# Wide maxima and full-height products in the second attention, and products of unused result in two stretches of waits

## What is computed

```
Q = query_seq @ Wq + bq;  K = ctx @ Wk + bk;  V = ctx @ Wv + bv      # 16 heads of width 16
scores = einsum('bhqd,bhkd->bhqk', Q, K) / sqrt(16)
attn = softmax(scores, axis=-1)
x = query_seq + einsum('bhqk,bhkd->bqhd', attn, V) @ Wo;  y = layernorm(x)
```

## Time and profile before

| | us |
|---|---|
| median of 3 runs (lowest, highest) | 940.2 (939.28, 941.24) |
| the profiled execution, its own time | 931.33 |
| its span, first to last instruction | 929.5 |
| TensorE busy | 847.6 (91%) |
| VectorE busy | 515.7 (55%) |
| ScalarE busy | 454.9 (49%) |
| mean granted TensorE clock | 0.965 |

### The profile page before, as it was taken

The page is one execution under the profiler, slowest core; times in us unless marked ns, Lnnn a source line. Parts: engine busy times, 40 slices in busy tenths (PEclk is TensorE's granted clock), DMA queues, the critical chain, the costliest instruction groups (busy, mean ns, idle before and its releaser), DMA issues.

```text
span 929.5 us, 10707 instructions
## 1 busy us (share of the span) xinstructions
PE 847.6 (91%) x4452; PEld 392.8 (42%) x4452; DVE 515.7 (55%) x714; ACT 454.9 (49%) x679; POOL 48.8 (5%) x41
## 2 busy tenths in 40 slices
PE   4989999989899999976899998999788989888987
PEld 2535444453434444542225435234355434554342
DVE  3479999633522012154745327359969595994442
ACT  3785222624254215334343342748885468752624
POOL 1000000300000000002100000000012000210000
PEclk9999999979999999997899899999899999999999
DMA  7000300000000000030000000000000000000011
GB/s 284 1 1 1 135 0 1 0 1 1 1 1 0 1 0 1 0 135 1 0 1 1 1 1 2 1 1 1 0 1 2 0 1 0 1 1 1 1 47 45
DMA packets 3006, 15.63 MB, mean 17 GB/s; under 512 B 656, under 2 KB 912, under 8 KB 2320
## 3 DMA queue, kind: packets, MB, share of 16 engines
q1 hardware_dynamic: 2816, 12.88, 3.5%
q0 software_dynamic: 144, 2.10, 0.6%
HBM read 12.87 MB, written 2.10 MB: 16 GB/s over the span
## 4 chain that ended last, share of the span: by engine, by line
PE 73%; ACT 14%; DVE 10%; issue 1%; DMA 1%; DVEq 0%; SPq 0%; POOL 0%; ACTq 0%
PE ps L412 71%; DVE VB L641 4%; ACT AR L628 3%; ACT AR L1822 2%; ACT AR L1812 1%; DVE AR L2118 1%; DMA CX<-in_ctxT 1%; ACT AR L1518 1%; DVE AR L653 1%; ACT AR L1788 1%; PE ps L587 1%; ACT AR L633 1%; ACT AR L631 1%; DVE AR L502 1%; ACT AR L1805 1%
## 5 line engine op out<-in xcount | busy, mean ns | idle before, releaser
L412 PE MATMUL ps<-AR,WA 128*128 128x512 f32 (+2 forms) x780 | 339.4, 596 | 5.0 <-DVE AR L2351 3.6
L412 PEld LDWEIGHTS ps<-AR,WA 128*128 128x128 f32 (+2 forms) x780 | 143.2, 189 | 187.1 <-issue 174.0
L412 PE MATMUL ps<-AR,CN 128*128 128x512 f32 (+3 forms) x320 | 113.8, 608 | 6.6 <-DVE AR L499 2.3
L412 PE MATMUL ps<-AR 128*64 128x128 f32 (+5 forms) x680 | 95.1, 401 | 9.7 <-DVE AR L2118 2.6
L653 DVE TENSOR_TENSOR AR<-ps,AR 128x512 f32<-128x512 f32 x24 | 16.6, 692 | 103.0 <-ACT AR L633 103.0
L628 ACT ACTIVATE AR<-ps 77x2048 f32<-77x2048 f32 x24 | 44.2, 1869 | 55.5 <-PE ps L412 55.3
L412 PEld LDWEIGHTS ps<-AR 128*64 128x64 f32 (+4 forms) x680 | 50.1, 158 | 46.5 <-issue 20.6
L412 PEld LDWEIGHTS ps<-AR,CN 128*128 128x128 f32 (+2 forms) x320 | 39.5, 163 | 59.0 <-issue 38.9
L641 DVE TENSOR_REDUCE VB<-ps 128x16 f32<-128x1232 f32 x32 | 44.5, 1438 | 32.3 <-PE ps L412 32.3
L412 PE MATMUL ps<-KB,WA 128*128 128x512 f32 (+1 forms) x120 | 52.9, 608 | 0.9 <-ACT AR L1805 0.9
L2248 DVE SCALAR_TENSOR_TENSOR AR<-AR,VC 128x512 f32<-128x512 f32 x72 | 50.6, 749 | 5.4 <-ACT AR L1746 4.4
(11 more groups left out here) (331 smaller groups left out, 1064.3 us busy)
## 6 DMA issues: line engine op xcount, KB each, us to landing
WA<-in_m SPq DMA_DIRECT2D x1, 2856.0 KB, 10.8
WA<-in_m SPq DMA_DIRECT2D x1, 2560.0 KB, 15.4
X<-in_xT POOLq DMA_DIRECT2D x1, 2048.0 KB, 9.1
WA<-in_m SPq DMA_DIRECT2D x1, 2048.0 KB, 9.7
out<-X SPq DMA_DIRECT2D x4, 512.0 KB, 3.1
WB<-in_m SPq DMA_DIRECT2D x1, 1024.0 KB, 5.2
AR<-in_rows SPq DMA_DIRECT2D x1, 640.0 KB, 9.8
WA<-in_m SPq DMA_DIRECT2D x1, 512.0 KB, 16.3
```

The costliest lines, as they stand in the source:

```text
L412: return nc.tensor.matmul(out, lhsT, rhs, start=first, stop=last)
```

## The change

Four edits, all on TensorE's list but one:

1. The maxima pass of "a2" takes the two zero-padded key tiles at once. A set (g, k) now covers two of the four blocks of tokens, 2k and 2k + 1, for both k of the keys: eight products of 32 rows with 154 columns in the place of sixteen with 77. VectorE's reduction reads the same 4 x 308 scores and writes its 16 results to other columns of `MXP`.
2. In that pass, from the second set on, one product of the full 128 rows with 204 columns is put between the wait for `att_mx` and the set's products. It writes the unused columns 308 to 511 of `bank(b, 0)`.
3. At the launch, three full-height products with 512 columns into bank 0 stand between the wait for the constants and that for the vectors.
4. In the second layer's head, `spare(n)` products (full height, n columns, bank 2, unused result) stand before the waits for `u5` (256, behind a wait for `kv_vs`), for `wu` (192), for `v_ln` (192) and for `ut` (256).

```
@@ attn_pe
                     else:
                         pe.wait_ge(*after("att_mx", nset(p, j, i - 1, b)))
+                        if PARTS[p] == 2:
+                            mm(bank(b, 0)[:, HALF:T], cn("ident"), CN[:, 0:T - HALF])
...
-                    for s in range(SUB):
+                    for s in range(2) if PARTS[p] == 2 else ():
+                        for r in range(4):
+                            row = slice(32 * r, 32 * r + 32)
+                            last = mm(bank(b, r)[:, 2 * s * M:2 * (s + 1) * M], qs[b][row, g, (2 * k + s) * P:(2 * k + s + 1) * P],
+                                      KF[row, :, g, b, :])
+                    for s in range(SUB) if PARTS[p] == 1 else ():
                         for r in range(4):
@@ attn_dve
-                    nc.vector.tensor_reduce(MXP[b].rearrange("p s (r n) -> p r s n", n=32)[:, :, :, i],
+                    where = MXP[b].rearrange("p s (r n) -> p r s n", n=32)
+                    nc.vector.tensor_reduce(where[:, :, :, i] if PARTS[p] == 1 else where[:, :, 2 * k:2 * k + 2, 2 * g:2 * g + 2],
@@ tensor, launch
             pe.wait_ge(*after("ld_cn", 16))
+            for n in range(3):
+                mm(ps[:, 0, :], cn("ident"), CN[:, 0:T])
             pe.wait_ge(*after("ld_vec", 16))
@@ tensor, head of the second layer
             last.then_inc(sem("h4_mm"), 1)
+
+            def spare(n):
+
+                mm(ps[:, 2, 0:n], cn("ident"), CN[:, 0:n])
+
+            pe.wait_ge(*after("kv_vs", LAYER["a2"] + 1))
+            spare(256)
             pe.wait_ge(*after("u5", 1))
             pe.wait_ge(*after("q3c", 1))
             mm(ps[:, 3, :], G6, U5).then_inc(sem("wu_mm"), 1)
+            spare(192)
             pe.wait_ge(*after("wu", 1))
...
+            spare(192)
             pe.wait_ge(*after("v_ln", 1))
             linear(0, 4)
...
             last.then_inc(sem("ut_mm"), 1)
+            spare(256)
             pe.wait_ge(*after("ut", 1))
```

## The result

| | before | after |
|---|---|---|
| median of 4 plain runs (lowest, highest), us | 939.74 (939.07, 941.24) | 931.89 (930.59, 932.25) |
| profiled execution, own time | 931.33 | 931.59 |
| its span | 929.5 | 929.8 |
| mean granted clock | 0.965 | 0.969 |

The ratio is 0.9912, 95% interval 0.9895 to 0.9929: the change takes 7.9 us off the median. The prediction had -5.1 us, to 935.1, in a range of 931.0 to 940.3.

The account below looks back on a forecast made before the run. TensorE, in flight 91% of the span, was taken to bound the kernel by its pace, clock dips and waits. Terms -0.68 - 4.00 - 2.0 + 1.6 = -5.1 us took 940.2 to 935.1 us, range 931.0 to 940.3.

Parts of the forecast that it names:

- Edit 1, the wide batch (0.55 us): Second attention's maxima pass: a wide batch takes 0.55 us against today's 0.89, so each half's first reduction starts 0.34 us sooner.
- Edit 2, the clock (-4.00 us): Second attention's first half: full-height products between sets hold the clock at 2.4 GHz, saving the dip's 4.00 us; bounds 0, -8.0.
- Edit 2, the round under the reduction (1.23 against 1.36): Maxima pass: TensorE's round with the full-height product takes 1.23 us, hidden under VectorE's reduction of 1.36 us.
- Both attention edits together (-4.7 us): Second attention: -0.68 us from wide products plus -4.00 us from the clock held by full-height products.
- rival C: Second attention: plain runs before lose the clock in both halves, so another -4.0 us, 931.1 us; chance 0.12.
- Edit 4 (-2.0 us): Second layer's head: spare products bring the clock back behind `wu_mm`, so `var_mm` gains 1.04 and `linear` 0.95 us.
- Edit 3 (+1.6 us): Launch: products end sooner, TensorE idles 2.5 us, and the first large products lose 1.6 us at low clock; bounds 0, +3.4.
- Rival B: Launch: the clock is kept for the first large products, so the +1.6 us falls away, 933.5 us; chance 0.18.
- The prediction's own signs: Wrong if reductions stand over 1.4 us apart, a maxima pass has clock 0.50, or the head's clock returns no sooner.
- rival D: Second attention: the clock falls in the maxima pass all the same, -0.5 us in all, 939.7 us; chance 0.16.
- The sum: Whole kernel: -0.68 - 4.00 - 2.0 + 1.6 = -5.1 us, taken off the plain runs' 940.2, giving 935.1 us.
- E: Maxima pass: TensorE bounds the rounds at 2.0 us against 1.36, so the kernel is slower, +3.3 us, 943.5 us; chance 0.08.

## Why the prediction held, step by step

- *Edit 1, the wide batch (0.55 us).* Right: 0.52 us. The first reduction came 0.33 us sooner in each half, as summed.
- *Edit 2, the clock (-4.00 us).* Right in kind: full clock in both halves in all seven traces with 204 or 150 columns between sets, a dip in the first half of all five without.
- *Edit 2, the round under the reduction (1.23 against 1.36).* Wrong, in two ways. The size: the full-height product was counted as 0.34 + 0.10 us, of which no row shows the 0.10, and puts the batch off by 0.54; with the batch's 0.81 (0.55 + 0.24 = 0.79 in the prediction) TensorE's round is 1.35 us. The criterion: TensorE's round was held against the reduction, and by that even 1.35 would be hidden. What the product lengthens is the chain from one reduction of a batch's banks to the next, 1.50 + 0.54 + 0.81 + 0.06 = 2.91 us for two rounds, or 1.46 each. Already with the prediction's own 0.44 and 0.79 that chain has 2.79 us, over the 2.72 of two reductions. It ate the 0.34 us of the first batch, and each half is at 15.07 us, not 14.4. The Trainium skill ("TensorE: Matmul & The Clock Gate", Part 3, "The mechanism") has weight loads pass a running matmul only in other row groups; worked out by that rule the prediction had 1.52 us for TensorE's round, where 1.35 is measured. Its 0.19 us for a load, which no row shows either, was too much; the rule itself agrees with the trace, in which the full-height product at 509.43 starts only when the batch of 508.62 is out after 0.81 us.
- *Both attention edits together (-4.7 us).* In the profile's comparison they give 33.50 - 30.14 = 3.4 us. On average over four traces it is 4.7, since the second half dips too in some executions. So the agreement with the forecast 4.7 is luck: a loss that was overlooked and a second dip that wasn't counted cancel. That is rival C in part; its full second -4.0 does not hold.
- *Edit 4 (-2.0 us).* Right in size on average, in mechanism only in part. From `h4_mm` to the first `maxima`: 18.25, 19.63, 18.25, 18.36, 18.25 and 16.92 us in the six traces without spares, mean 18.3; 17.30, 15.06, 16.35, 16.99, 14.96, 16.35, 17.30 and 17.30 in the eight with, mean 16.5. So -1.8 us, and -0.95 in the first trace after. The forecast had the clock back behind `wu_mm`, for `var_mm` and `linear`. `linear` took 1.14 us in all eight traces with spares and 2.09 in all six without; but `var_mm` ran at full clock in four of the eight, partly with the head's edit alone (1.76 us), and at 2.07 or 2.08 us in three. In two of the eight `wu_mm` too was at full clock (1.13 us). It was so as well in two traces without spares, and there `var_mm` was back at 2.08. So what the spares do is in some executions to bring the clock back and in others to keep it. That each dense stretch had brought the clock back was also read too generally: in the same trace TensorE was in flight 10.15 of 10.60 us without its coming back.
- *Edit 3 (+1.6 us).* Right in size where it strikes: the first large products took 18.99 to 23.92, 4.93 us, against 3.54 before, and 5.11 in the second trace of the changed kernel, so +1.4 and +1.6. It struck in two of the three traces with the launch products alone in front of them. Rival B, no loss, is the third. In the whole times the loss isn't shown: 1.0025 beside 1.0015 for the kernel before again, and 0.9905 beside 0.9902.
- *The prediction's own signs.* It called itself wrong where the reductions stand over 1.4 us apart; they do, at 1.36 and 1.55 by turns, and so that step failed, although the time lies in the range. `maxima` comes 440.40 - 426.12 = 14.28 us after `wu_mm`'s start before and 442.90 - 429.57 = 13.33 after, 0.95 sooner and not 2.0. The eight first large products were to take more than 6 us, which doesn't fit its own term of +1.6 on their 3.70; they took 5.09. And the chance of "within", 0.15, is less than the 0.16 of rival D alone, which lies in it.
- *The sum.* -5.1 against -7.9 us measured. The step at fault is the base: it was summed on an execution with fewer dips than usual, and carried over to the median unchanged. The places on average over the traces give -4.7 - 1.8 and +1.0 for the launch (two losses in three traces), so -5.5 us; single traces of before and after give only -3.4 - 0.95 + 1.4 = -2.9. By the parts timed alone, the head's edit is -4.0 (within -1.5 to -6.5) where its own place shows -1.8, and the attention's -5.4 where its place shows -4.7. Whether the rest is chance or dips that these edits spare further on stays open: the executions of one program differ by up to 13 us (931.59 to 944.55), and one trace of each is not enough to say.
- Rivals D (the clock falls all the same) and E (TensorE's rounds become so long that the kernel is slower) are out. That the rounds grow past the reduction is there, at 1.46 us and not 2.0, but by the chain and not by TensorE alone; only with the narrow products is the round, 1.61 us, TensorE's own.

## What to carry to other kernels

Where two stretches do the same work and one is at half clock, their difference prices the dip, and the idle times next to it show where to try products of unused result. Make room first and then fill it: both halves took 31.96 us with the wide products alone, 33.27 with filling alone and 30.15 with both. (The whole times, 0.9961, 0.9966 and 0.9943, have intervals that overlap.) Where two engines hand the same buffers to and fro, add up the whole chain from one use of a buffer to the next, and not only each engine's own work: here it was 2.91 us although either engine had only 2.7. Profile a kernel whose clock moves more than once, and compare stretches between two events in several traces, not spans. Warming the array ahead of a wait of 2.9 us gained nothing here.

## What the runs showed of the hardware

- TensorE with a matmul in flight almost all the time stayed at 1.2 GHz: 10.15 of 10.60 us in 32-row products. One full-height product with 150 or 204 columns ahead of each batch went with full clock in all 14 halves traced with it; with 96 columns one half of four had a mean clock of 0.60.
- A full-height float32 product between 32-row batches puts them off by 0.39 us with 96 columns, 0.45 with 150 and 0.54 with 204. 54 more columns cost 0.06 us, the next 54 cost 0.09. Two rounds then take 2.76, 2.82 and 2.91 us, each time 1.50 + 0.81 + 0.06 us and the delay.
- One program's executions spread from 931.59 to 944.55 us (35 runs of the kernel before on one chip), with mean granted clocks from 0.946 to 0.965. The two traces of it differ in where the dips lie and in how many there are.
